# Loading the first row first, mask factors on 128 partitions on GpSimd, and list numbers converted inside the block loop

## The chip, the cores and the metric

One core of a Trainium2 chip runs one program. The metric is the device time of one execution in microseconds (us), as a median over runs. The engines are TensorE (PE in the profile; PEld is its weight load), VectorE (DVE), ScalarE (ACT), GpSimd (POOL) and SyncE (SP), which here only issues DMAs. They run side by side and wait for one another on semaphores.

## The reference, cut to what matters

x has 4 batch rows of 512 tokens and 128 features.

```python
x = x + 0.5 * ffn0(layernorm(x))        # 2 layers: local attention + gated FFN
x = x + attn(layernorm(x))              # 16 heads, with a mask of sines
x = x + 0.5 * ffn0(layernorm(x))        # the same weights again
x = x + 0.5 * mixture(x)                # 8 experts, 2 for each token, and a shared one
x = x + ttt(x)                          # two steps of training at test time
x = x + 0.5 * mixture(x)
```

Each head of `attn` adds 0.3 * log(sigmoid(val / temperature) + 1e-6) to its scores, with

```python
pos = arange(L) / L * 2 * pi
val = sin(pq) * cos(pk) + sin(pk) * cos(pz) + sin(pz) * cos(pq) - threshold
# pq = pos_q + phase[0],  pk = pos_k + phase[1],  pz = (pos_q + pos_k) / 2 + phase[2]
```

By the addition theorems val is a product of six rows of 512 for the queries and six for the keys of a head: the mask factors. They depend only on the 16 heads' phases and on sines and cosines of the positions, which are loaded as a table.

## The kernel before

x is kept transposed, features on partitions, tokens along the free axis. The stages run in the order load, ffn0, attn, ffn1, moe0, ttt, moe1. Each engine has its own list of instructions, in program order, and every stage begins with a wait for x_ready, which is raised when a row of x is finished in the stage before.

**Semaphores.** Counters start at START = 1. GpSimd raises every semaphore by one at the beginning, in alphabetical order; a wait for START + n is satisfied only after that and n increments.

**The start.** SP issues the loads in the order phase, pos, acol, aw, bv_row, xT, con, fcol, wqkv, rot, wo, w1, w2 (`load_sync`), then waits for the mask factors (mask_rows), stores them to DRAM (mask_q, mask_k), and issues the late loads and the filling of the mixtures' lists. VectorE (`load_dve`) runs `mask_factors`: twelve small instructions on the angles of the 16 heads, a sine on ScalarE (`load_act`, L1129), and then some 21 instructions of 512 columns on 16 partitions; after that the constants (`mean_w` from con, L1059; bf16 copies), and x_ready. The factors lie in the arena, the memory that ffn0 needs, so GpSimd's `ffn_zero_pads` (L1006 to L1014) and VectorE's ffn0 wait until both are stored (mask_stored). TensorE and ScalarE wait for the pads (pads_zero).

**ffn0.** Row 0 is normalised: the mean (`ln_mean`, L266), centring (L296), square, variance (L271), Ln and Exp for 1/std, scaling (L301). ScalarE makes the rounded part of wqkv for layer 0 (L718, ahead of the square), VectorE the rest (`low(0)`, L908). Then h_hi and h_lo, and the projections (`product`, L318 to L320), with rotation on VectorE (L760), squares on ScalarE, sums on GpSimd (`summed`, L938; `rotated`, L947 and L949) and the scaling (`scaled`, L773). ScalarE's copy for layer 1 comes before the first squares, VectorE's `low(1)` after the last scaling, and TensorE's first scores after that; `maxima` (L787) reads them. From there rows follow each other in a pipeline.

**attn.** SP loads, for each pass of two heads, the mask factors (L1319 and L1320, six rows of 512 each) and then the split queries and keys. TensorE multiplies the factors (L1401); the first pass can begin only when they are there, later ones are loaded a pass ahead.

**The mixture.** Tokens are scattered into blocks of 128, sorted by expert, and SP loads the 39 blocks in four groups, XGROUPS = ((0, 3), (3, 15), (15, 27), (27, 39)), a semaphore each (xg0_loaded to xg3_loaded). Column 128 of a block holds the number of the token slot to which its result goes. VectorE converts those numbers to integers for all four groups (L1963) and then begins the loop over blocks, whose first instruction clips the gate of block 0 (L1971). TensorE turns block j and projects it (L1711 to L1713); in turning block 3 it waits for group 1. GpSimd scatters the results with the numbers (L2031).

Of the kernel before, what the change touches and what calls it, by code (L numbers as in the profile page):

```python
# [25 lines left out]
P = 128  # L26
# [21 lines left out]
MF = 6  # L48

# [70 lines left out]
def position_tables():  # L120

    pos = (np.arange(L, dtype=np.float32) / np.float32(L) * np.float32(2 * np.pi)).astype(np.float64)
    t = np.stack([np.sin(pos), np.cos(pos), np.sin(pos / 2), np.cos(pos / 2)])
    return np.tile(t[None], (NH, 1, 1)).astype(np.float32)
# [17 lines left out]
def build(nc, I, out, stop=None):  # L142
    ctx = ExitStack()
    with ctx:
# [22 lines left out]

        PS = ctx.enter_context(nc.psum_tensor("PS", [P, 8, 512], F32))
# [3 lines left out]
        mq_dram = nc.dram_tensor("mask_q", (NH, MF, L), F32).ap()  # L172
        mk_dram = nc.dram_tensor("mask_k", (NH, MF, L), F32).ap()
# [64 lines left out]
        w2 = carve([DEPTH, 3, D])  # L238
        stage_memory(big)
# [149 lines left out]
        def ffn_pe(pe, f):  # L389
# [192 lines left out]
            pe.wait_ge(s("low_by_dve"), START + FFN_SPLITS * (f + 1))  # L582
            scores(0, 0)
# [9 lines left out]
        def ffn_act(act, f):  # L593
# [120 lines left out]
            if f:  # L714
                act.wait_ge(s("ffn_loaded"), START + 64)
# [3 lines left out]
            ln_act(e_input(f, 0), 3)  # L719
            entered(0)  # L720
            for w, hi, _ in weights[1:]:
                act.activation(hi, w, ACT.Copy).then_inc(s("weights_high"), 1)
            for j in range(PAIRS + 1):
                if j < PAIRS:
                    squares(0, j)
                if j:
                    rnorm(0, j - 1)
            exponentials(0, 0)
# [7 lines left out]
        def ffn_dve(v, f):  # L736
# [164 lines left out]
            if f:  # L901
                v.wait_ge(s("ffn_loaded"), START + 64)
# [7 lines left out]
            ln_centre(xT[:, 0, :], e_input(f, 0), 3)  # L910
            low(0)
            ln_scale(e_input(f, 0), c_one, c_zero, y[:, 0, :])
            entered(0)
            for j in range(PAIRS + 1):
# [4 lines left out]
            low(1)  # L919
            maxima(0, 0)  # L920
# [96 lines left out]
        stage_memory()  # L1017
        pos = carve([4, L])
        m_q = carve([MF, L])
        m_k = carve([MF, L])  # L1020
        m_t = carve([6, L])
        ang, turns, ang_f, sc = (carve([8]) for _ in range(4))
        turns_i = turns.bitcast(I32)
        phase = carve([8])
# [1845 lines left out]
```

## Time and profile before

| what | value |
|---|---|
| median of 3 runs | 2316.15 us (2303.26 to 2316.34) |
| profiled execution, its own time | 2330.29 us |
| its span, first to last instruction | 2328.1 us |
| mean granted TensorE clock | 0.890 of full |
| PE, DVE, ACT, POOL busy | 81%, 66%, 53%, 46% |
| chain that ended last | PE 34%, DVE 7%, ACT 6%, issue 5%, POOL 4%, DMA 2% |

The profile is of one execution, and its own time lies beside its span; the runs are executions without it. Busy shares are means over stages that have different limits. The chain is followed back from the last instruction to what released each step.

### The profile page before, as it was taken

Reading aid. Unit: us, or ns where it says so; the run is one execution under the profiler, and the core shown is the slowest. Engines: PE = TensorE matmul, PEld = TensorE weight load, DVE = VectorE, ACT = ScalarE, POOL = GpSimd, SP = SyncE. Lnnn points to the kernel's source line nnn. Section 1 sums busy time; section 2 is a strip of 40 time slices with the busy share of each in tenths; the row PEclk is TensorE's granted clock in tenths of the full one; section 3 lists DMA queues with packets and bytes.
Section 4 is the critical chain, followed back from the end, with each engine's and each line's share of the span. In section 5 each row is a group of like instructions: output and inputs, shape, how many; then the busy total and the mean of one; then the engine's idle time right before and its main releaser. Section 6 shows DMA issues by size and latency. Waiting matters only on the chain.

```text
span 2328.1 us, 42531 instructions
## 1 busy us (share of the span) xinstructions
PE 1876.3 (81%) x14557; PEld 1177.2 (51%) x14620; DVE 1547.5 (66%) x2455; ACT 1226.8 (53%) x2826; POOL 1062.6 (46%) x838
## 2 busy tenths in 40 slices
PE   2799999859898889569999985399569999884696
PEld 1456665424555555245556652288234554633485
DVE  5687778456979987468887864478445455426485
ACT  2467766437979997346667655144332332334242
POOL 2466566334767776346666551523223133005233
PEclk9799999876979997679999997699779999995797
DMA  6000000020000001000000003200400000000202
GB/s 230 1 1 2 2 2 1 1 92 13 25 19 21 22 26 44 10 1 2 2 2 2 2 2 111 79 19 22 150 0 0 1 0 0 1 0 27 63 23 70
DMA packets 43934, 63.40 MB, mean 27 GB/s; under 512 B 7504, under 2 KB 33488, under 8 KB 42736
## 3 DMA queue, kind: packets, MB, share of 16 engines
q1 hardware_dynamic: 39232, 51.96, 7.2%
q0 software_dynamic: 4544, 9.35, 1.2%
q8 instruction: 97, 1.59, 0.3%
q14 instruction: 61, 0.50, 0.1%
HBM read 45.26 MB, written 21.18 MB: 29 GB/s over the span
## 4 chain that ended last, share of the span: by engine, by line
PE 34%; DVE 7%; ACT 6%; issue 5%; POOL 4%; DMA 2%; SPq 0%; DVEq 0%; ACTq 0%; POOLq 0%
PE PS L1729 3%; POOL sorted_x L2024 3%; PE PS L1711 2%; PE PS L448 2%; ACT arena L635 1%; PE PS L1712 1%; PE PS L1713 1%; PE PS L2350 1%; PE PS L1719 1%; PE PS L2321 1%; PE PS L2367 1%; PE PS L2363 1%; DVE arena L760 1%; PE PS L2297 1%; PE PS L2371 1%
## 5 line engine op out<-in xcount | busy, mean ns | idle before, releaser
L1503 POOL TENSOR_TENSOR arena<-arena 128x1024 f32<-128x1024 f32 x128 | 299.6, 2362 | 144.2 <-ACT arena L1437 144.2
L635 ACT ACTIVATE arena<-PS,arena 128x128 f32<-128x128 f32 x512 | 180.2, 370 | 120.3 <-DVE arena L787 119.9
L955 POOL TENSOR_TENSOR arena<-arena 128x512 f32<-128x512 f32 x128 | 132.4, 1040 | 225.8 <-DVE arena L794 223.9
L1411 PE MATMUL PS<-con,arena 128*128 128x128 f32 x1024 | 163.5, 307 | 45.4 <-DVE arena L1487 44.0
L318 PE MATMUL PS<-arena_r 128*128 128x512 f32 x216 | 120.6, 558 | 92.5 <-DVE arena_r L1924 43.6
L760 DVE SCALAR_TENSOR_TENSOR arena<-PS,fcol,big 128x512 f32<-128x512 f32 x256 | 177.4, 741 | 15.8 <-PE PS L320 9.1
L1411 PEld LDWEIGHTS PS<-con,arena 128*128 128x128 f32 x1024 | 124.4, 155 | 121.1 <-issue 96.5
L1437 ACT ACTIVATE arena<-PS,arena 128x512 f32<-128x512 f32 x256 | 154.9, 688 | 56.3 <-DVE arena L1468 54.5
L1487 DVE COPY arena<-PS 128x512 f32<-128x512 f32 x256 | 166.2, 684 | 24.9 <-PE PS L1411 24.8
L1448 ACT ACTIVATE arena<-arena 128x512 f32<-128x512 f32 x256 | 162.6, 636 | 23.3 <-DVE arena L1475 17.2
L2031 POOL DMA_INDIRECT expert_y<-arena x78 | 74.7, 957 | 207.6 <-DVE arena L1990 203.9
L1468 DVE TENSOR_REDUCE arena<-PS 128x4 f32<-128x2048 f32 x64 | 146.6, 2291 | 29.3 <-PE PS L1393 29.3
L938 POOL TENSOR_TENSOR arena<-arena 128x512 f32<-128x512 f32 x64 | 109.3, 1708 | 67.6 <-ACT arena L611 30.8
L611 ACT ACTIVATE arena<-PS 128x512 f32<-128x512 f32 x128 | 74.1, 593 | 110.3 <-PE PS L320 77.0
L448 PE MATMUL PS<-arena 32*64 32x128 f32 x4096 | 131.6, 278 | 0.0
L1825 ACT ACTIVATE big<-big 128x512 f32<-128x512 f32 x78 | 49.3, 632 | 155.7 <-DVE big L1971 155.7
L448 PEld LDWEIGHTS PS<-arena 32*64 32x64 f32 x4096 | 115.7, 136 | 28.4 <-issue 28.4
L2465 POOL TENSOR_TENSOR arena<-arena 128x512 f32<-128x512 f32 x32 | 40.7, 1273 | 171.9 <-DVE arena L2412 171.8
L773 DVE SCALAR_TENSOR_TENSOR arena<-arena 128x512 f32<-128x512 f32 x128 | 116.2, 954 | 4.5 <-ACT arena L621 4.5
L787 DVE TENSOR_REDUCE arena<-PS 128x4 f32<-128x512 f32 x128 | 82.1, 682 | 50.1 <-PE PS L448 49.4
L318 PEld LDWEIGHTS PS<-arena_r 128*128 128x128 f32 x216 | 44.3, 205 | 133.6 <-DVE arena_r L1620 39.7
L635 ACT ACTIVATION_READ_ACCUMULATOR arena<-PS,arena 128x1 f32 x512 | 107.1, 209 | 0.0
(373 smaller groups left out, 4714.2 us busy)
## 6 DMA issues: line engine op xcount, KB each, us to landing
big<-in_gu SPq DMA_DIRECT2D x16, 512.0 KB, 8.4
sorted_x<-in_slots SPq DMA_DIRECT2D x2, 2515.5 KB, 14.5
arena<-sorted_x SPq DMA_DIRECT2D x6, 774.0 KB, 7.4
big<-in_dn SPq DMA_DIRECT2D x16, 256.0 KB, 8.7
arena<-expert_y SPq DMA_DIRECT2D x16, 256.0 KB, 3.3
big<-in_wqkv SPq DMA_DIRECT2D x2, 1536.0 KB, 8.6
arena<-q_split SPq DMA_DIRECT2D x96, 32.0 KB
arena<-k_split SPq DMA_DIRECT2D x96, 32.0 KB
```

Of the source, the lines that this page charges most:

```text
L318: pe.matmul(bank, w_hi, hi, start=first, stop=False)
L448: mm = pe.matmul(PS[w * WINDOW:(w + 1) * WINDOW, par, t * P:(t + 1) * P], qs[h, i, a:a + WINDOW], keys, start=False, stop=half == 1, skip_ ...
L635: act.activation(pr[:, u % 2, t, :], PS[:, u % 2, t * P:(t + 1) * P], ACT.Exp, bias=nmax[:, u % 2, t:t + 1], accum_out=psum_[:, u % 2, t:t ...
L760: v.scalar_tensor_tensor(t_prod[:, j % 2, 2 * half + i, :], PS[:, pair_bank(r, j) + half, :], fcol[:, layer, kind + half:kind + half + 1], ...
L773: v.scalar_tensor_tensor(dst, t_rn[:, j % 2, :], 1e12, t_rot[:, j % 2, half, :], ALU.min, ALU.mult).then_inc(s("qk_scaled"), 1)
L955: g.tensor_tensor(pn[:, u % 2, :, :], pr[:, u % 2, :, :], pinv[:, u % 2, :].unsqueeze(2).broadcast_to([P, TPB, P]), ALU.mult).then_inc(s(" ...
L1411: tr = pe.transpose(PS[:, 4 + t % 2, kt * P:(kt + 1) * P], pp[:, st % 2, t, kt * P:(kt + 1) * P], ident)
L1437: act.activation(pp[:, st % 2, t, :], PS[:, t, :], ACT.Exp, bias=a_nmax[:, st % 2, t:t + 1]).then_inc(s("a_exp"), 1)
L1448: act.activation(z, z, func, bias=bias, scale=scale).then_inc(s("mask_stage"), 1)
L1468: v.tensor_reduce(a_nmax[:, st % 2, :], PS[:, 0:TPB, :], AX.X, ALU.max, negate=True).then_inc(s("a_nmax"), 1)
L1487: v.tensor_copy(ppT[:, :, t * P:(t + 1) * P], PS[:, 4 + t % 2, :].rearrange("p (a b) -> p a b", a=TPB)).then_inc(s("ppT_ready"), 1)
L1503: g.tensor_tensor(a, a, mk[:, hp, 2 * half:2 * half + 2, :], ALU.mult).then_inc(s("a_masked"), 1)
```

## The change

Five edits, in the start and in the mixture.

1. `load_sync` loads row 0 of x, phase and pos first (first_loads), then layer 0 of wqkv and con (con_loaded), fcol and rot (rot_loaded), then layer 1 of wqkv, rows 1 to 3 of x, wo, w1 and w2 (ffn_loaded), then the attention's columns. SP raises 83 semaphores (LATE) to START itself; GpSimd raises 17 others (FIRST) before the remaining ones. `mean_w` becomes a memset.
2. phase and pos are laid out on 128 partitions: 16 heads x 8 chunks of 64 positions (CHUNKS, CW). VectorE keeps the twelve angle steps (`mask_angles`), then raises x_ready; ScalarE's sine follows; GpSimd computes the factors after the pads (`mask_factors(g)`), in 27 instructions of 64 columns, ahead of its first sum of ffn0. The factors lie in `big`, behind the weights, and no longer in the arena, so nothing of ffn0 waits for their store. In DRAM they are stored by chunk, and attention loads them in pieces of 64.
3. The waits of ffn0's first row are spread: TensorE takes the mean after first_loads and waits for pads, constants and con_loaded only before the projections; VectorE's `load_consts` stands between centring and `low(0)`; rot_loaded is waited for before the rotation, ffn_loaded before the first scores.
4. ScalarE squares before it copies layer 0 of wqkv, and copies layer 1 after the last rnorm. The columns from acol (`attn_consts`) are computed on VectorE before the first maxima.
5. In the mixture, the numbers of group g are converted in the block loop at block a + 1, where a is the group's first block.

```diff
-            sp.dma_start(phase[0:NH, :], I["phase"]).then_inc(s("phase_loaded"), 16)
-            sp.dma_start(pos[0:NH, :, :], I["pos"]).then_inc(s("phase_loaded"), 16)
...
+            sp.dma_start(xT[:, 0, :], I["xT"][:, 0, :]).then_inc(s("first_loads"), 16)
+            sp.dma_start(phase, I["phase"]).then_inc(s("first_loads"), 16)
+            sp.dma_start(pos, I["pos"]).then_inc(s("first_loads"), 16)
+            sp.dma_start(wqkv[:, 0, :], I["wqkv"][:, 0, :]).then_inc(s("con_loaded"), 16)
+            sp.dma_start(con[:], I["con"]).then_inc(s("con_loaded"), 16)
...
+            for name in LATE:
+                sp.sem_inc(s(name), START)
+            sp.wait_ge(s("mask_rows"), START + 1)
...
-            if f == 0:
-                g.wait_ge(s("mask_stored"), START + 32)
...
             if f == 0:
+                pe.wait_ge(s("first_loads"), START + 48)
             ln_pe(xT[:, 0, :], e_input(f, 0), 3, 3)
+            if f == 0:
+                pe.wait_ge(s("pads_zero"), START + 6)
+                pe.wait_ge(s("consts"), START + 7)
+                pe.wait_ge(s("con_loaded"), START + 32)
...
+            if f == 0:
+                ln_square(e_input(f, 0))
+                act.wait_ge(s("con_loaded"), START + 32)
             for w, hi, _ in weights[:1]:
                 act.activation(hi, w, ACT.Copy).then_inc(s("weights_high"), 1)
...
+            if f == 0:
+                act.wait_ge(s("ffn_loaded"), START + 80)
+                for w, hi, _ in weights[1:]:
+                    act.activation(hi, w, ACT.Copy).then_inc(s("weights_high"), 1)
             exponentials(0, 0)
...
             ln_centre(xT[:, 0, :], e_input(f, 0), 3)
+            if f == 0:
+                load_consts(v)
             low(0)
...
             low(1)
+            if f == 0:
+                attn_consts(v)
             maxima(0, 0)
...
             def angle_sum(dst, t, a, x, b, y, op):
-                then(v.tensor_scalar(t, a, x, None, ALU.mult))
-                then(v.scalar_tensor_tensor(dst, b, y, t, ALU.mult, op))
+                g.tensor_scalar(u, b, y, None, ALU.mult).then_inc(s("mask_step"), 1)
+                steps[0] += 1
+                then(g.tensor_scalar(t, a, x, None, ALU.mult))
+                then(g.tensor_tensor(dst, u, t, op))
...
-                sp.dma_start(mq_st[hp][0:MF], mq_dram[bass.ds(h, 1), :, :].rearrange("a f n -> (a f) n")).then_inc(s(f"factors{hp}_loaded"), 16)
+                sp.dma_start(mq_st[hp][0:MF].rearrange("f (c n) -> f c n", c=CHUNKS), mq_dram[bass.ds(h, 1), :, :, :].rearrange("a c f n -> f (a c) n")).then_inc(s(f"factors{hp}_loaded"), 16)
...
-            for g, (a, z) in enumerate(XGROUPS):
+            def block_ids(g):
+                a, z = XGROUPS[g]
                 v.wait_ge(s(f"xg{g}_loaded"), START + 16 * (m + 1))
                 v.tensor_copy(ids_u[:, a:z], xg[:, a:z, D]).then_inc(s("ids_ready"), 1)
...
+            turned_in(0)
+            turned_in(1)
             for u in range(NBLK + 3):
+                for g, (a, z) in enumerate(XGROUPS):
+                    if u == a + 1:
+                        block_ids(g)
...
                     ffn_zero_pads(g, f)
+                    if f == 0:
+                        mask_factors(g)
                     ffn_pool(g, f)
```

## Rows read from the trace of the kernel before

**Rows 1.** Busy time by stretch, the start: bounds, length, busy (count), granted clock, DMA, GB/s.
```profile
core 0: us, PE busy (x) PEld busy (x) DVE busy (x) ACT busy (x) POOL busy (x), PEclk, DMA share, GB/s
0.00:32.00 32.00, 0.00 (x0) 0.00 (x0) 15.86 (x52) 1.49 (x2) 1.40 (x10) 1.00 0.67 220
```

**Rows 2.** Timeline of the start: start us, us, engine, line, operation [idle before, releaser].
```profile
2.12 0.43 SPq L1031 DMA_DIRECT2D aw<-in_aw  x1
...
3.54 0.43 SPq L1033 DMA_DIRECT2D con<-in_con  x1
...
9.12 0.16 DVE L1082 COPY arena<-arena 16x3 f32<-16x3 f32 x1 [8.07 <-POOLq L2787]
...
11.59 0.21 ACT L1129 ACTIVATE arena<-arena 16x6 f32<-16x6 f32 x1 [9.56 <-DVE arena L1094]
...
30.68 0.15 POOL L1006 MEMSET arena<- 128x65 f32 x1 [30.24 <-DMA mask_k<-arena]
...
32.32 2.05 PE L266 MATMUL PS<-xT,mean_w 128*128 128x512 f32 x2 [32.32 <-POOL arena L1013]
...
33.57 1.48 ACT L718 ACTIVATE arena_r<-big 128x1536 fp32r<-128x1536 f32 x1
...
35.11 1.75 DVE L908 TENSOR_TENSOR big_r<-big,arena_r 128x1536 fp32r<-128x1536 f32 x1
...
39.40 0.75 DVE L301 SCALAR_TENSOR_TENSOR ln_scaled<-ln_centered,col,ln_rstd 128x512 f32<-128x512 f32 x1 [2.54 <-ACT ln_rstd L287]
...
42.87 0.77 PE L318 MATMUL PS<-arena_r 128*128 128x512 f32 x1 [4.88 <-issue]
...
47.08 1.28 POOL L938 TENSOR_TENSOR arena<-arena 128x512 f32<-128x512 f32 x1 [14.91 <-issue]
```

**Rows 3.** Timeline of the first mixture, where its block loop begins.
```profile
1503.05 0.17 DVE L1963 CAST arena<-arena 128x12 uint32<-128x12 f32 x1 [0.70 <-DMA arena<-sorted_x]
...
1503.62 0.63 PE L1713 MATMUL PS<-big_r,arena_r 128*128 x1
...
1508.39 0.17 DVE L1963 CAST arena<-arena 128x12 uint32<-128x12 f32 x1 [2.44 <-DMA arena<-sorted_x]
1508.48 0.69 DVE L1971 TENSOR_SCALAR big<-PS 128x512 f32<-128x512 f32 x1
```

**Rows 4.** Busy time by stretch, two stretches of attention's loop, columns as in rows 1.
```profile
540.00:560.00 20.00, 19.94 (x114) 11.14 (x114) 12.30 (x13) 14.07 (x25) 12.21 (x6) 0.50 0.03 6
580.00:600.00 20.00, 16.96 (x174) 10.14 (x173) 18.10 (x23) 19.09 (x34) 14.81 (x7) 1.00 0.10 27
```

**Rows 5.** DMA issues of the first 80 us: count, KB, us from issue to landing.
```profile
con<-in_con SPq DMA_DIRECT2D x1, 527.5 KB, 6.5
...
aw<-in_aw SPq DMA_DIRECT2D x1, 256.0 KB, 2.7
```

**Rows 6.** GpSimd's instructions by shape, whole span: count, busy us, mean ns, idle before.
```profile
L1503 POOL TENSOR_TENSOR arena<-arena 128x1024 f32<-128x1024 f32 x128 | 299.6, 2362 | 144.2 <-ACT arena L1437 144.2
L955 POOL TENSOR_TENSOR arena<-arena 128x512 f32<-128x512 f32 x128 | 132.4, 1040 | 225.8 <-DVE arena L794 223.9
...
L2282 POOL TENSOR_TENSOR arena<-arena 128x1024 f32<-128x1024 f32 x4 | 7.6, 1912 | 42.8 <-ACT arena L2177 42.8
...
L1009 POOL CAST arena_r<-arena 128x65 fp32r<-128x65 f32 x4 | 0.8, 237 | 0.1
```

**Rows 7.** Timeline of ffn0's first row: VectorE beside GpSimd, alone, and before maxima.
```profile
57.61 3.42 DVE L773 SCALAR_TENSOR_TENSOR arena<-arena 128x512 f32<-128x512 f32 x2 [0.68 <-ACT arena L621]
...
58.77 1.71 POOL L949 TENSOR_TENSOR arena<-arena 128x512 f32<-128x512 f32 x1
...
67.97 1.29 DVE L773 SCALAR_TENSOR_TENSOR arena<-arena 128x512 f32<-128x512 f32 x2 [0.20 <-ACT arena L621]
...
75.69 1.29 DVE L787 TENSOR_REDUCE arena<-PS 128x4 f32<-128x512 f32 x2 [4.77 <-PE PS L448]
```

**Rows 8.** Timeline of the start of attention's loop.
```profile
515.30 0.29 SPq L1320 DMA_DIRECT2D arena<-mask_k  x1
...
517.09 2.04 PE L1401 MATMUL PS<-arena 6*128 6x512 f32 x2 [15.11 <-DMA arena<-mask_k]
```

More of the change, by code:

```diff
@@ L238, in build @@
         w2 = carve([DEPTH, 3, D])
+        pos = carve([4, CW])
+        m_q, m_k = carve([MF, CW]), carve([MF, CW])
+        m_t = carve([6, CW])
+        ang, turns, ang_f, sc, phase = (carve([8]) for _ in range(5))
+        turns_i = turns.bitcast(I32)
         stage_memory(big)
@@ L582, in ffn_pe @@
             pe.wait_ge(s("low_by_dve"), START + FFN_SPLITS * (f + 1))
+            pe.wait_ge(s("ffn_loaded"), START + 80)
             scores(0, 0)
@@ L901, in ffn_dve @@
             if f:
-                v.wait_ge(s("ffn_loaded"), START + 64)
+                v.wait_ge(s("ffn_loaded"), START + 96)
             weights = ffn_weights()
@@ L1055, in load_dve, with load_consts @@
                 v.memset(col[:, i:i + 1], val).then_inc(s("columns"), 1)
-            mask_factors(v)
+            v.memset(mean_w[:], 1.0 / D).then_inc(s("consts"), 1)
+            mask_angles(v)
             v.wait_ge(s("columns"), START + 7)
-            v.wait_ge(s("first_loads"), START + 80)
-            v.tensor_scalar(mean_w[:], ones, 1.0 / D, None, ALU.mult).then_inc(s("consts"), 1)
+            v.tensor_copy(col[:, 7:8], c_one).then_inc(s("x_ready"), B)
+        def load_consts(v):
+            v.wait_ge(s("con_loaded"), START + 32)
             v.tensor_copy(ident_b[:], ident).then_inc(s("consts"), 1)
@@ L1080, in mask_factors @@
             two_pi_lo = float(2 * np.pi - two_pi_hi)
-            v.wait_ge(s("phase_loaded"), START + 32)
-            then(v.tensor_copy(ang[h, 0:3], phase[h, 0:3]))
-            then(v.tensor_scalar(ang[h, 3:6], phase[h, 0:3], pi / 2, None, ALU.add))
-            then(v.tensor_scalar(ang_f[h, 0:6], ang[h, 0:6], 1.0 / (2 * pi), None, ALU.mult))
-            then(v.tensor_copy(turns_i[h, 0:6], ang_f[h, 0:6]))
-            then(v.tensor_copy(ang_f[h, 0:6], turns_i[h, 0:6]))
+            v.wait_ge(s("first_loads"), START + 48)
@@ L1090, in mask_factors @@
             for op, bound, turn in ((ALU.is_gt, pi, -two_pi_hi), (ALU.is_lt, -pi, two_pi_hi)):
-                then(v.tensor_scalar(ang_f[h, 0:6], ang[h, 0:6], bound, turn, op, ALU.mult))
-                then(v.tensor_tensor(ang[h, 0:6], ang[h, 0:6], ang_f[h, 0:6], ALU.add))
-            then(v.tensor_scalar(ang[h, 0:6], ang[h, 0:6], 3.1415925, -3.1415925, ALU.min, ALU.max))
-            v.tensor_copy(sc[h, 6:7], ang[h, 0:1]).then_inc(s("angles"), 1)
-            v.wait_ge(s("sines"), START + 1)
@@ L1096, in mask_factors @@
-            s0, s1, s2, c0, c1, c2 = (sc[h, i:i + 1] for i in range(6))
-            sa, ca, sh, ch = (pos[h, i, :] for i in range(4))
-            def angle_sum(dst, t, a, x, b, y, op):
-                then(v.tensor_scalar(t, a, x, None, ALU.mult))
-                then(v.scalar_tensor_tensor(dst, b, y, t, ALU.mult, op))
-            t = m_t[h, 5, :]
-            sin_q, cos_q, sin_z, cos_z, sin_k = m_q[h, 0, :], m_t[h, 1, :], m_t[h, 2, :], m_q[h, 1, :], m_t[h, 4, :]
+                then(v.tensor_scalar(ang_f[:, 0:6], ang[:, 0:6], bound, turn, op, ALU.mult))
@@ L2785, in _ @@
         def _(g):
-            for name in sorted(set(sems) - {"x_scattered", "y_scattered"}):
-                g.sem_inc(sems[name], START)
+            names = [n for n in sorted(sems) if n not in FIRST + LATE + ("x_scattered", "y_scattered")]
+            for name in FIRST + tuple(names):
+                g.sem_inc(s(name), START)
             for st in run:
```

146 lines of the change are left out of this document (92 added, 54 removed).

## Prediction

> **What bounds the kernel now.** I read four views, in this order. The table of busy time by stretch comes first: in the first 32.0 us TensorE does nothing (x0) and VectorE is busy for half [rows 1]. So the 81% of TensorE over the whole span says nothing about the start, and what is saved there is saved in full, since each later stage waits for the x of the one before it.
>
> The timeline of the start says what those 32 us are [rows 2]. VectorE's first piece of the mask factors stands until 9.12 us, and what released it is GpSimd's queue: GpSimd raises every semaphore to START in alphabetical order, and phase_loaded comes late in it. Sines follow at 11.59, then the 512-wide factors on 16 partitions, their store, and only when mask_k has landed (30.24) does GpSimd zero the pads from 30.68. TensorE's first layer-norm matmul starts at 32.32, the first projection at 42.87, GpSimd's first sum of squares at 47.08.
>
> The third view is the timeline at the first mixture [rows 3]. The half-row of block 0 that is clipped first has its last matmul at 1503.62 + 0.63 = 1504.25, but the clip (L1971) starts at 1508.48, because VectorE stands in the list-number casts of groups 1 to 3; the last of them starts at 1508.39, released by its load. Group 1, which TensorE needs for block 3, was there at 1503.05. The second mixture repeats this.
>
> The fourth is the table by stretch inside attention, for the noise [rows 4]. Two stretches of 20 us with the same loop: granted clock 1.00 (2.4 GHz) with 23 VectorE instructions, granted 0.50 (1.2 GHz) with 13. A low stretch so costs about 20 x (1 - 13/23) = 8.7 us.
>
> **The change, part by part.** Times are on the profiled execution: 2330.29 us, span 2328.1.
>
> *First row first.* The new gate is first_loads: row 0 of x, phase, positions, 0.40 MB, the first three issues; its START is GpSimd's first increment instead of about its hundredth. In the trace, aw is the load with 0.39 MB up to and with it: issued 2.12, landed 2.7 later, 4.8 us [rows 2, 5]. I take 4.8. The upper bound is con, with 2.0 MB up to it: 3.54 + 6.5 = 10.0 (if the loads issued behind share the engines with the first ones). The angle steps stay on VectorE, 12 small instructions, 11.59 - 9.12 = 2.5 us, whose length hardly hangs on 16 or 128 partitions; x_ready follows them, so TensorE's mean starts at about 7.4 instead of 32.3. From there to the first projection it was 42.87 - 32.32 = 10.55 us, and the chain (mean, square, variance, rstd, scale, halves) is the same. So 18.0 without disturbance.
>
> *Waits that are added in it.* con_loaded (weights of layer 0 and con, 1.7 MB up to it) lands before 10.0 by the con row. ScalarE reaches it after its square at about 11, with the weight copy and rstd queued behind it; VectorE reaches it after the centring at 10.3, with low(0) and the scaling behind. Zero cost, at most 2 us if the loads are slower than con's. low(0) loses its lead: the copy (1.48, L718) now comes after the square, so low(0), 1.75 us, ends about 0.3 before the scaling can start, where it had 39.40 - 36.86 = 2.5 to spare. rot_loaded and ffn_loaded (6 MB in all) are needed at about 20 and 48; by 32.0 us the core had moved 220 GB/s x 32 us = 7.0 MB [rows 1]. Zero.
>
> *Mask factors on GpSimd.* 27 instructions of 64 columns on 128 partitions, after the pads (1.6 us, 30.68 to 32.3), so from 9.0. No row shows a TENSOR_SCALAR on GpSimd. From the rows [rows 6]: a 65-wide cast 0.24; a two-input one, from 1040 ns at 512 and 1912 at 1024, 1.70 ns a column, 0.28 at 64. The 17 one-input ones at 0.24 and 10 two-input ones at 0.28 make 6.9 us. Twenty of them are waited for; VectorE's 13 angle instructions of 0.16 fill 2.47 us, a gap of 0.03, and I take twice that, 1.2. Together 8.1 us, done at 17.1. It must be done by the first sum, 4.2 us after the projection.
>
> *VectorE beside it.* Two two-input operations in SBUF take 1.29 us when GpSimd is idle and 3.42 beside GpSimd's adds of 1.28 to 1.71 us [rows 2, 7]: each loses 1.07, close to one GpSimd instruction. On the path, about six VectorE instructions (low(0), scale, add, cast, two subtractions) can meet GpSimd; with GpSimd's instructions a quarter of a us long, 6 x 0.25 = 1.5 us. Lower bound 0; upper bound all the GpSimd work still to come when low(0) starts, 8.1 - 3.4 = 4.7. The projection so comes at 19.5, and the prologue gives 42.87 - 19.5 = 23.4. GpSimd is held up in turn, at most by low(0) and all from the scaling to the projection, 1.75 + (42.87 - 39.40) = 5.2 us, and six small casts of con at the 0.17 of rows 3, 1.0: done by 23.3 at worst, needed at 23.7. Hidden, barely.
>
> The Trainium skill (SBUF — State Buffer, section Who interferes with whom) speaks against this part: a VectorE operation with two SBUF inputs and a GpSimd operation that reads SBUF lock each other out, one whole instruction at a time. By that rule six instructions wait at most one short GpSimd instruction each, an estimated 1.7 us together, and 1.7 would stand in place of the 4.7 as the bound: the sum would be -31.1 at worst of this part, not -28.1. The rows point the same way (1.07 lost beside adds of 1.28), but with long instructions only.
>
> *Layer 1's weights later.* ScalarE's copy (1.48) now starts after the last rnorm, at the time of VectorE's last two scalings (1.29): low(1) and the first scores come 0.2 later (0 to 1.5). The three tiny acol instructions stand before maxima, where VectorE waits 4.77 us for TensorE anyway [rows 7]; without that cover they cost 0.5.
>
> *SP.* 83 increments and later mask stores on its queue: the stores move from 25 to about 20, the late loads behind them too, and nothing before attention at 515 asks for them. The factor loads become 256-byte pieces, 48 instead of 6 each. At attention's start TensorE waits for mask_k, 515.30 to 517.09 [rows 8]: I add 0.3 (0 to 1.8, the wait doubled). Later passes load a pass ahead.
>
> *Mixtures.* The clip goes from 1508.48 to 1504.3: 4.2 each, 8.4 together; the loop behind it is a chain of blocks, so it is kept. What stands behind a cast in VectorE's queue now is a clip, and behind that TensorE; the casts of groups 1 to 3 come at blocks 4, 16 and 28, when their loads (the last at 1508.39) are long there or, for block 4, three blocks old. Four casts of 0.17 cost at most 0.7 per mixture, if VectorE is the late one. Bounds per mixture 3.5 to 5.6: TensorE also loses a stall of some 4 us and may reach the high clock a block or two sooner.
>
> Sum: -23.4 + 0.2 + 0.3 - 8.4 = -31.3. 2330.29 becomes 2299.0. The median of the runs shown lies 14.1 below the profiled execution, less than two low stretches of rows 4; taken off it, 2316.15 - 31.3 = 2284.9, say 2285.
>
> **Rivals.** *The prologue gives less.* GpSimd is late for its first sum: the price decides from (23.7 - 9.0)/27 = 0.54 us an instruction. At 1.04 (the 512-wide adds of L955) it is done at 37, 13 late, and the result is 2298. A first load at 10.0 instead of 4.8 gives 2290. For it: no TENSOR_SCALAR row, the tight slack. Against: the 0.24 of the cast.
>
> *The mixture gives nothing*, because the first blocks then wait for something else (group 1 in turn_in, a cast): 2293. Against: group 1 was there at 1503.05.
>
> *Slower.* One mechanism: GpSimd's 27 factor instructions, in the place before its first sum. At 1.71 each (L949 beside VectorE) they end at 55.2, 31.5 late, and the whole gain is eaten; above that the kernel is slower. At the dearest row, 2.36 (L1503), they end at 72.7, 49 late: 2334. Against: that is the price of 1024 columns, here there are 64. That the change doesn't do what it says is the same case, the wait for the mask moved from VectorE to GpSimd.
>
> **How the numbers follow.** Forecast 0.72, less prologue 0.17, no mixture 0.05, slower 0.03; 0.03 for more than bounds allow. The range joins the sum's own bounds (-36 to -24: the 4.7, 1.8, 1.5 and the casts one way, no disturbance and a sooner clock the other) and one low stretch more or less, some 8 us: 2270 to 2300, which takes in the first two rivals. A change under 1%, 23 us, is what a measurement here hardly tells from none; the forecast is 1.35%, so a low stretch or two can bring it below. Of the forecast's 0.72 some 0.65 stays above 1%, of the first two rivals half, of the rest up 0.03: faster 0.79, same 0.19, slower 0.02.
>
> **What would show it.** Right: TensorE's first matmul at 7 to 8, first projection at 18 to 21, GpSimd's factors done before its first sum, first clip in each mixture within 5 us of the first list load. Wrong: GpSimd busy with factors when ScalarE's squares are done; first_loads later than 6; con_loaded ending ScalarE's wait; the interval from projection to attention longer than in rows 2 to 8; TensorE waiting for xg1.

## The result, and the profile after

The changed kernel takes 2274.9 us (median of 4 runs, 2272.9 to 2277.3), beside 2315.8 for the kernel before (2303.3 to 2316.3): ratio 0.9837, 95% interval 0.9802 to 0.9872. That ratio is the one of the mean times, which lie 37.8 us apart; the two medians lie 40.9 apart. The forecast was 2285, range 2270 to 2300, a gain of 31.3. The direction, the range and both mechanisms held; 6.5 us of the 37.8 are not in the forecast, and the experiments are mostly about them.

The stretch that answers to [rows 1], busy time by stretch of the changed kernel's start, same columns: TensorE works 14.40 of the 32 us instead of none, and GpSimd 22.63 instead of 1.40.

```profile
0.00:32.00 32.00, 14.40 (x32) 7.70 (x32) 18.84 (x46) 11.01 (x15) 22.63 (x43) 1.00 0.70 251
```

The timeline of the same start answers to [rows 2].

```profile
5.04 0.17 DVE L1135 COPY big<-big 128x3 f32<-128x3 f32 x1 [3.83 <-DMA big<-in_pos]
...
7.62 2.04 PE L288 MATMUL PS<-xT,mean_w 128*128 128x512 f32 x2 [7.62 <-DVE col L1105]
...
9.25 0.45 POOL L1164 TENSOR_SCALAR big<-big 128x64 f32<-128x64 f32 x1
...
12.53 1.76 DVE L949 TENSOR_TENSOR big_r<-big,arena_r 128x1536 fp32r<-128x1536 f32 x1 [1.13 <-ACT arena_r L750]
12.54 2.05 POOL L1166 TENSOR_SCALAR big<-big 128x64 f32<-128x64 f32 x1
14.66 0.88 DVE L323 SCALAR_TENSOR_TENSOR ln_scaled<-ln_centered,col,ln_rstd 128x512 f32<-128x512 f32 x1 [0.38 <-ACT ln_rstd L309]
...
18.74 0.77 PE L340 MATMUL PS<-arena_r 128*128 128x512 f32 x1 [5.50 <-issue]
...
21.74 1.09 ACT L640 ACTIVATE arena<-PS 128x512 f32<-128x512 f32 x2 [4.90 <-PE PS L342]
...
23.72 0.15 POOL L1185 MEMSET big<- 128x64 f32 x1
23.83 1.27 POOL L987 TENSOR_TENSOR arena<-arena 128x512 f32<-128x512 f32 x1
```

The first matmul moved from 32.32 to 7.62, the first projection from 42.87 to 18.74, 24.1 earlier, and GpSimd's first sum from 47.08 to 23.83, 23.25 earlier. The last three lines show the 0.9 us between these two: ScalarE's first squares are done at 22.83, and the sum starts the moment the last factor instruction is done, without idle time before it. TensorE's projection would have let it start at 18.74 + 4.21 = 22.95, with the 4.21 of [rows 2].

The forms of GpSimd between 9 and 24 us, which answer to the prices of [rows 6]:

```profile
L1166 POOL TENSOR_SCALAR big<-big 128x64 f32<-128x64 f32 x6 | 4.8, 806 | 0.0
L1164 POOL TENSOR_SCALAR big<-big 128x64 f32<-128x64 f32 x6 | 3.5, 585 | 0.6
L1167 POOL TENSOR_TENSOR big<-big 128x64 f32<-128x64 f32 x6 | 2.0, 329 | 0.5
...
L1183 POOL COPY big<-big 128x64 f32<-128x64 f32 x1 | 0.2, 237 | 0.1
```

A TENSOR_SCALAR of 64 columns in the angle sums (L1164, L1166) is nearly twice as dear as a copy of that size, 0.43 to 0.45 us where nothing meets it, and one of them stands 2.05 us.

The timeline of the first mixture answers to [rows 3]: the first projection (L1773), the last matmul of the first half-row (L1775), the clip (L2037), the first cast (L2026), now behind the clip, and the next transpose.

```profile
1459.48 0.79 PE L1773 MATMUL PS<-arena_r 128*128 x1
...
1460.49 0.63 PE L1775 MATMUL PS<-big_r,arena_r 128*128 x1
...
1461.16 0.69 DVE L2037 TENSOR_SCALAR big<-PS 128x512 f32<-128x512 f32 x1 [1.94 <-PE PS L1775]
...
1462.92 0.16 DVE L2026 CAST arena<-arena 128x3 uint32<-128x3 f32 x1
...
1463.15 0.45 PE L1760 MATMUL PS<-con,arena 128*128 128x128 f32 x1 [0.75 <-DVE arena_r L2020]
```

In the kernel before, the first projection and the next transpose of the same place:

```profile
1502.61 0.79 PE L1711 MATMUL PS<-arena_r 128*128 x1
...
1510.47 0.45 PE L1698 MATMUL PS<-con,arena 128*128 128x128 f32 x1 [4.93 <-DVE arena_r L1958]
```

The clip comes right behind that matmul, as its releaser says, instead of 4.2 us after it. From the first projection to the next transpose it is 1463.15 - 1459.48 = 3.67 us, and was 1510.47 - 1502.61 = 7.86: 4.2 less. In the second mixture the same two instructions stood at 2170.61 and 2178.31 and stand at 2121.16 and 2124.83: 4.0 less. From the clip of block 0 to that of block 38 it takes 118.3 to 119.3 us in the traces of the two kernels that convert all numbers up front (before, and prologue only, below) and 117.5 to 119.3 in those of the list-number edit alone and of the changed kernel, so what is won at the first clip is neither lost nor multiplied in the loop.

The start of attention, for [rows 8]: from the issue of mask_k's load to the first mask matmul 2.16 us instead of 1.79. In the other traces of kernels that load these factors in pieces at this place it is 1.86 to 2.14, so the pieces cost 0.1 to 0.4 us.

```profile
487.53 0.28 SPq L1382 DMA_DIRECT2D arena<-mask_k  x1
...
489.69 2.04 PE L1463 MATMUL PS<-arena 6*128 6x512 f32 x2 [15.50 <-DMA arena<-mask_k]
```

And two stretches in attention, for [rows 4]; the loop still has stretches at 0.50 with few VectorE instructions and stretches near 1.00 with many:

```profile
540.00:560.00 20.00, 18.74 (x109) 10.12 (x108) 12.79 (x13) 11.20 (x21) 9.11 (x5) 0.50 0.04 9
560.00:580.00 20.00, 17.77 (x169) 10.80 (x168) 17.64 (x22) 16.45 (x30) 13.34 (x6) 0.93 0.09 24
```

So the sum of the places that the edits touch is 23.25 + 4.2 + 4.0 - 0.4 = 31.1 us in the two traces, against 31.3 forecast and 37.8 measured.

### The profile page after: what moved, and what is told of

It reads as the page before. It is cut to its first block, busy times and chain, and to the rows that moved or that the text cites. A ratio compares the mean times of both kernels' runs of the same rounds, so it can differ in the third digit from the quotient of the medians.

```text
span 2275.5 us, 42539 instructions
## 1 busy us (share of the span) xinstructions
PE 1850.7 (81%) x14557; PEld 1165.6 (51%) x14620; DVE 1530.8 (67%) x2433; ACT 1227.7 (54%) x2826; POOL 1078.4 (47%) x865
## 4 chain that ended last, share of the span: by engine, by line
PE 35%; DVE 9%; issue 6%; ACT 6%; POOL 1%; DMA 1%; DVEq 0%; SPq 0%; ACTq 0%; POOLq 0%
PE PS L1791 3%; PE PS L1773 2%; PE PS L470 2%; PE PS L1775 2%; PE PS L1774 2%; PE PS L2416 1%; DVE arena L801 1%; PE PS L1781 1%; PE PS L2387 1%; ACT arena L664 1%; PE PS L2433 1%; PE PS L2429 1%; PE PS L2363 1%; PE PS L2437 1%; PE PS L504 1%
## 5 line engine op out<-in xcount | busy, mean ns | idle before, releaser
L664 ACT ACTIVATE arena<-PS,arena 128x128 f32<-128x128 f32 x512 | 180.7, 370 | 119.6 <-DVE arena L828 119.3
L1473 PE MATMUL PS<-con,arena 128*128 128x128 f32 x1024 | 157.2, 298 | 48.4 <-DVE arena L1549 46.0
L1473 PEld LDWEIGHTS PS<-con,arena 128*128 128x128 f32 x1024 | 118.8, 150 | 121.4 <-issue 94.6
L814 DVE SCALAR_TENSOR_TENSOR arena<-arena 128x512 f32<-128x512 f32 x128 | 111.1, 914 | 5.1 <-ACT arena L650 5.1
```

Source lines behind the costliest of these rows:

```text
L664: act.activation(pr[:, u % 2, t, :], PS[:, u % 2, t * P:(t + 1) * P], ACT.Exp, bias=nmax[:, u % 2, t:t + 1], accum_out=psum_[:, u % 2, t:t ...
L1473: tr = pe.transpose(PS[:, 4 + t % 2, kt * P:(kt + 1) * P], pp[:, st % 2, t, kt * P:(kt + 1) * P], ident)
```

## The experiments

The theory: each edit gives what its own stall was, and the rest of the 37.8 comes from TensorE's granted clock, whose mean differs from run to run. The rivals: the mixtures give the rest; the two edits together give more than each alone; the rest of the prologue (waits, load order) gives it.

To tell the clock from the edits I use the span and mean granted clock of every run. With the two levels of [rows 4], 1.00 and 0.50, the time at the low one is span x (1 - clock) / 0.5: of a run with 2293.9 and 0.905, it is 436 us. Over the 122 runs of the kernel before, the changed kernel and the eleven variants below, a straight line with one slope for all and a level for each row of the table fits to 2.0 us (the first comparison's runs of before, whose clocks are not known, are left out). Its slope is 0.354 us of run time for each us at the low clock; that is a fit over runs, and none of them set the clock. The last column is a kernel's level on this line at 450 us of low time, good to about 1 us.

| kernel | median us (runs) | ratio to before, 95% | mean low time, us | level at 450 us low |
|---|---|---|---|---|
| before, the runs beside the variants | 2306.4 (44) | | 458 | 2304.9 |
| changed, first runs | 2274.9 (4) | 0.9837 (0.9802 to 0.9872) | 444 | 2277.0 |
| changed, beside four variants | 2273.0 (6) | 0.9846 (0.9807 to 0.9884) | 435 | 2277.9 |
| list numbers only | 2295.6 (12) | 0.9960 (0.9934 to 0.9985) | 442 | 2299.7 |
| prologue only | 2284.0 (6) | 0.9909 (0.9885 to 0.9932) | 446 | 2284.1 |
| start held back | 2293.7 (9) | 0.9958 (0.9934 to 0.9982) | 434 | 2300.3 |
| alphabetical increments | 2283.5 (4) | 0.9879 (0.9826 to 0.9932) | 455 | 2282.3 |
| factors on VectorE | 2278.2 (4) | 0.9857 (0.9803 to 0.9910) | 435 | 2283.1 |
| factors twice | 2284.0 (10) | 0.9894 (0.9862 to 0.9927) | 451 | 2285.2 |
| x_ready early, factors split | 2268.8 (6) | 0.9849 (0.9820 to 0.9877) | 436 | 2273.9 |
| mask loads early | 2263.7 (4) | 0.9824 (0.9749 to 0.9898) | 423 | 2273.3 |
| both early | 2254.7 (4) | 0.9774 (0.9713 to 0.9835) | 398 | 2270.3 |
| TensorE kept busy | 2273.5 (5) | 0.9864 (0.9825 to 0.9903) | 434 | 2282.1 |
| both early, kept busy | 2260.4 (4) | 0.9804 (0.9764 to 0.9843) | 419 | 2271.8 |

The level is no clean measure of an edit: where TensorE's waiting itself lies at the low clock, taking it away takes low time away too, and the line books 0.354 of that to the clock. Both places are named below. The ratio and its interval come from all runs, and are not the quotient of the two medians. With four to six runs the interval is some 11 to 34 us wide, so few of these edits can be told apart by their medians; what follows rests on the traces and on the levels.

**List numbers only.** The kernel before with this edit alone:

```diff
-            for g, (a, z) in enumerate(XGROUPS):
+            def block_ids(g):
+                a, z = XGROUPS[g]
                 v.wait_ge(s(f"xg{g}_loaded"), START + 16 * (m + 1))
                 v.tensor_copy(ids_u[:, a:z], xg[:, a:z, D]).then_inc(s("ids_ready"), 1)
-                if g == 0:
-                    turned_in(0)
-                    turned_in(1)
+
+            turned_in(0)
+            turned_in(1)
             for u in range(NBLK + 3):
+                for g, (a, z) in enumerate(XGROUPS):
+                    if u == a + 1:
+                        block_ids(g)
```

> The kernel before with only the list-number edit. Theory (each edit gives what its own stall was, and the 6.5 us beyond the forecast come from where TensorE's low clock falls in attention): the two mixtures give the 4.3 and 3.1 us read from the two traces, 7.4 together, so 2308 from a median of 2316, give or take the 8 us of one low stretch. Rival (the excess comes from the mixtures, which are worth all that the start does not give, 37.8 - 23.3 = 14.5): 2301.

Measured: 2295.6, below both forecasts, which started from 2316. It is 11.2 below the 2306.8 of the 20 runs of before beside it; the interval is 3.5 to 15.2 and holds the theory's gain and the rival's. The timeline of the first mixture shows the same clip as in the changed kernel, 1.68 us behind the projection's start:

```profile
1478.68 0.79 PE L1711 MATMUL PS<-arena_r 128*128 x1
...
1480.36 0.69 DVE L1975 TENSOR_SCALAR big<-PS 128x512 f32<-128x512 f32 x1 [1.94 <-PE PS L1713]
...
1482.35 0.30 PE L1698 MATMUL PS<-con,arena 128*128 128x128 f32 x1 [0.75 <-DVE arena_r L1958]
```

The 3.67 us from projection to transpose are 7.86 in the kernel before, as in the changed one. The level falls by 5.2. Here a part is booked to the clock, as busy time by stretch of the kernel before shows, one stretch of 2 us in the stall of each mixture:

```profile
1506.00:1508.00 2.00, 0.00 (x0) 0.00 (x0) 0.00 (x0) 0.00 (x0) 0.00 (x0) 1.00 0.90 217
...
2174.00:2176.00 2.00, 0.00 (x0) 0.00 (x0) 0.00 (x0) 0.00 (x0) 0.00 (x0) 0.50 0.80 193
```

No engine works in either, and the second stall lies at 0.50, the first only at its ends. So between 4.0 and 8.2 us of low time go with the stalls, 1.4 to 2.9 at 0.354, and 6.6 to 8.1 in all. Of the 14.5 that the rival needed, the place itself shows none beyond 8.2; the median alone would not have told them apart.

**Prologue only.** The changed kernel with the first diff turned round.

> The changed kernel with the list numbers converted up front again, as in the kernel before. Theory (as for the run of the list-number edit alone): 2275 + 7.4 = 2282, and 23 to 33 below the kernel before. Rival (the excess comes from the mixtures): 2275 + 14.5 = 2289. Rival (the two edits are not additive, because a moved start shifts where the low clock falls): any time further than 8 us from 2282.

Measured: 2284.0, 22.8 below before (interval 15.7 to 26.5), level 20.8 below. 22.8 and 11.2 are 34.0 in the medians, against the 33.8 of both edits in the next run; the levels give 20.8 + 5.2 = 26.0 against 27 to 28. So the two edits add, as far as 2 us at equal clock can be told from none.

**The changed kernel beside them.**

> The changed kernel once more, beside the others on one chip. Theory (the 37.8 us of the first comparison were 6 us too many, because the runs of the kernel before that it was held against lay high: 2316 there, 2307 in the 20 runs beside the single edits): the gain is 21 + 9 to 11 = 30 to 32, 0.987. Rival (the two edits together give more than each alone): 36 us and more, 0.984 or less.

Measured: 2273.0, 33.8 below the 2306.9 of the 17 runs beside it, interval 26.8 to 44.5. That lies between the theory's 30 to 32 and the rival's 36, and the interval holds both. But the kernel before has been run 44 times by now: 2298.9 to 2327.8, median 2306.4, where the four runs of the first comparison had 2315.8. Against 2306.4, the 2274.9 and 2273.0 are gains of 31.5 and 33.4, nearer to the theory.

**Start held back.** One instruction and its wait in the changed kernel, ahead of the angle steps:

```diff
+            v.memset(arena[:, 0:27000], 0.0).then_inc(s("columns"), 1)
+            v.wait_ge(s("columns"), START + 8)
             mask_angles(v)
-            v.wait_ge(s("columns"), START + 7)
```

> The changed kernel with one VectorE memset of 27000 columns ahead of the angle steps, so that TensorE's first matmul should come near 32 us instead of 7.6, as in the kernel before; all else stays. Theory (the start is on the path in full): the time grows by the same 24 us, to 2299, give or take one low stretch of 8, and that is 9 below the kernel with the list-number edit alone, which would then be what the rest of the prologue and the clock give. Rival (later stages wait for something else, a load or a store, so that the start is worth less than its length): under 2290.

```profile
6.79 22.56 DVE L1103 MEMSET arena<- 128x27000 f32 x1 [5.57 <-issue]
...
31.95 2.04 PE L288 MATMUL PS<-xT,mean_w 128*128 128x512 f32 x2 [31.95 <-DVE col L1106]
...
516.54 2.04 PE L1464 MATMUL PS<-arena 6*128 6x512 f32 x2 [15.46 <-DMA arena<-mask_k]
```

Everything starts 24.3 us later (the projection at 43.02), as late as in the kernel before, and attention's first mask matmul, 516.54 instead of 489.69, is 26.9 later. Measured: 2293.7, 19 to 21 above the two medians of the changed kernel, level 22.8 above (2277.5, the mean of its two, here and below). It lies where the list-number edit alone lies (2295.6, levels 2300.3 and 2299.7). So the start is worth 19 to 23 of its 24.3 us at the end, and of the prologue nothing but its earlier start gives anything that can be seen beside the 1 us of a level: the rival that waits and load order gave the rest is out.

**Alphabetical increments.** The changed kernel without FIRST and LATE:

```diff
-            for name in LATE:
-                sp.sem_inc(s(name), START)
...
-            names = [n for n in sorted(sems) if n not in FIRST + LATE + ("x_scattered", "y_scattered")]
-            for name in FIRST + tuple(names):
+            for name in sorted(set(sems) - {"x_scattered", "y_scattered"}):
                 g.sem_inc(s(name), START)
```

> The changed kernel with every semaphore raised by GpSimd in alphabetical order again, as in the kernel before, so that x_ready comes last. Theory (the order of these increments is a part of the gain by itself): the queue that reached phase_loaded at 9.1 us in the kernel before reaches x_ready at 12 to 14, the first matmul moves from 7.6 to there, and the end with it: 2279 to 2282. Rival (the loads and the angle steps set the start, the increments are hidden): first matmul below 8.5, 2275 to 2276.

```profile
12.40 2.04 PE L288 MATMUL PS<-xT,mean_w 128*128 128x512 f32 x2 [12.40 <-POOLq L2852]
```

The first matmul at 12.40 is released by GpSimd's queue, 4.8 later; the level is 4.8 higher, the median 8.6 to 10.5, above the 2279 to 2282 expected. The order and place of these increments were worth some 5 us of the gain.

**Factors on VectorE.**

```diff
             mask_angles(v)
+            mask_factors(v)
...
-                    if f == 0:
-                        mask_factors(g)
```

> The changed kernel with the 27 factor instructions of 64 columns on VectorE, right behind the angle steps and ahead of x_ready, none on GpSimd. Theory (a GpSimd instruction of this size costs 0.54 us with its wait, a VectorE one about 0.2 by the angle steps, but all of it stands on the path here): the first matmul 5.5 to 6.5 later, at 13.1 to 14.1, the first sum 0.9 less late and the scaling undisturbed, so the first sum 3.5 to 5 later and the time 2279 to 2280. Rival (contention between VectorE and GpSimd costs the changed kernel more than its own rows show): 2275 or less.

```profile
14.08 2.05 PE L288 MATMUL PS<-xT,mean_w 128*128 128x512 f32 x2 [14.08 <-DVE col L1106]
...
25.00 0.77 PE L340 MATMUL PS<-arena_r 128*128 128x512 f32 x1 [5.29 <-issue]
...
29.22 1.28 POOL L987 TENSOR_TENSOR arena<-arena 128x512 f32<-128x512 f32 x1 [13.63 <-issue]
```

The first matmul comes 6.5 later and the first sum 5.4; the level is 5.6 higher, the median 3 to 5. This run also prices the contention: with GpSimd idle, mean to projection takes 25.00 - 14.08 = 10.92; beside its factors, 18.74 - 7.62 = 11.12. Sharing cost VectorE's chain 0.2 us. The 10.92 is itself 0.37 above the 10.55 of the kernel before, and what adds that is open.

**Factors twice.** (The second time overwrites the first with the same numbers.)

```diff
...
-                        mask_factors(g)
+                        mask_factors(g, 0)
+                        mask_factors(g, 1)
```

> The changed kernel with GpSimd computing the mask factors twice over, 27 more instructions of 64 columns before its first sum of squares. Theory (GpSimd's factors stand on the path, since they end 0.9 us after the first sum could run): 27 at 0.44 to 0.54 us, the first sum at 36 to 38 instead of 23.8, and the end later by the same 12 to 14.6: 2287 to 2290. Rival (the lateness is absorbed by the 11 us in which GpSimd waits behind row 0's sums): the first sum moves, the end does not: 2275 to 2279.

```profile
34.48 1.26 POOL L987 TENSOR_TENSOR arena<-arena 128x512 f32<-128x512 f32 x1
...
499.94 2.04 PE L1466 MATMUL PS<-arena 6*128 6x512 f32 x2 [15.20 <-DMA arena<-mask_k]
```

The first matmul of this execution is at 6.65, so the first sum comes 27.8 behind it instead of 16.2: the second 27 took 0.43 us each. From the first matmul to attention's first mask matmul it is 499.94 - 6.65 = 493.3 us in this trace, and 479.9 to 482.2 in three traces with the factors computed once (the changed kernel's two and prologue only): 11.1 to 13.4 more, so close to all of the 11.6 arrives there, and the 11 us in which GpSimd later waits don't absorb it. Measured 2284.0, between theory and rival, 9 to 11 above the changed kernel, and the level 7.7 above. The rest of the 11.6 may be booked to the clock: up to attention this trace has some 70 us of low time against some 60, 3.5 at the slope of the line. GpSimd is on the path here, though at 0.43 an instruction, not the 0.54 of the theory's upper end.

**x_ready early, factors split.**

```diff
-            sp.wait_ge(s("mask_rows"), START + 1)
+            sp.wait_ge(s("mask_rows"), START + 2)
...
-            mask_angles(v)
             v.wait_ge(s("columns"), START + 7)
             v.tensor_copy(col[:, 7:8], c_one).then_inc(s("x_ready"), B)
+            mask_angles(v)
...
                     if f == 0:
-                        mask_factors(g)
+                        mask_factors(g, 0)
...
+            if f == 0:
+                mask_factors(g, 1)
             for r in range(ROWS):
```

> The changed kernel with x_ready raised before the angle steps, so that TensorE's mean runs beside them, and with the mask factors in two parts: four of the six angle sums before GpSimd's first sum of squares, the other 15 instructions behind row 0's sums, where GpSimd stood idle from 44 to 55 us. Theory (GpSimd's factors are 0.9 us late for the first sum, and the angle steps cost 2.3 on the path): first matmul at 5.1, first projection at about 17, first sum 2 to 3 us sooner than 23.83; 2272. Rival (the lateness is hidden by what follows, or the second part gets in VectorE's way): 2275 or more.

```profile
17.15 0.76 PE L340 MATMUL PS<-arena_r 128*128 128x512 f32 x1 [5.31 <-issue]
...
21.37 1.28 POOL L987 TENSOR_TENSOR arena<-arena 128x512 f32<-128x512 f32 x1 [5.22 <-issue]
```

GpSimd now waits 5.22 us for its first sum, which stands 4.22 behind the projection, as it did before the change. It is 2.46 sooner; the level is 3.6 lower, the median 4 to 6. That speaks against the rival, but doesn't rule it out: the interval of this run, 2265 to 2278, reaches its 2275, and attention's first mask matmul at 487.67 lies where three traces with the unsplit factors have it, 487.5 to 489.7.

**Mask loads early.** The last lines of the profile after show another wait: TensorE is idle for 15.5 us at attention's start, and the load that ends it stands in SP's queue behind the stores of the split keys. The first pass's factor loads go ahead of row 2's stores:

```diff
             for b in range(B):
+                if b == 2:
+                    sp.wait_ge(s("mask_stored"), START + 32)
+                    for hp in range(HEADS_PER_PASS):
+                        load_mask_factors(sp, 0, hp)
...
-            sp.wait_ge(s("mask_stored"), START + 32)
...
-                load_mask_factors(0, hp)
```

> The changed kernel, but the two heads' mask factors for attention's first pass are loaded while the projections of rows 2 and 3 run, instead of behind the last store of the split keys. Theory (at attention's start TensorE waits for mask_k alone, 483.4 to 489.7 us): its first mask matmul comes 5 to 6 us sooner, near 484, and as the heads land near 492, before the four mask quarters are through, the end comes 5 to 6 sooner: 2268 to 2269. Rival (the heads' loads, still behind the stores, are then what ends last): 2 or less, 2272 to 2274.

```profile
480.42 2.04 PE L1464 MATMUL PS<-arena 6*128 6x512 f32 x2 [9.61 <-DVE arena L1345]
```

The wait is now for VectorE's last values and 9.61 long instead of 15.50. Median 2263.7, 9 to 11 below the changed kernel, but over four runs from 2247 to 2280; the level falls by 4.2, somewhat short of the 5 to 6 expected.

**Both early.** The last two diffs together.

> The kernel with x_ready raised early and the factors split, with the early loads of mask factors on top. Theory: the two gains add, 3.5 and 5 to 6 at equal time at the low clock, so 2264 to 2265 and the fastest of all. Rival: the loads gain nothing and it stays at 2269.

Measured: 2254.7, ratio 0.9774 (0.9713 to 0.9835), level 2270.3: 52 below the kernel before, 18 to 20 below the changed one, and the fastest kernel here. Only 7 of these 18 to 20 stand at equal low time; the other part goes with 37 to 46 us less of it. Whether that is owed to the edits, or is luck of four runs, is open.

**TensorE kept busy.** The changed kernel, with work that no one reads in the gap at attention's start:

```diff
         def attn_pe(pe):
+            for _ in range(12):
+                pe.matmul(PS[:, 7, :], mean_w[:], xT[:, 0, :], start=True, stop=True)
```

> The changed kernel with 12 matmuls of 128x512 (mean_w with row 0 of x, into bank 7, which the first mask matmul then overwrites) between the last projection and attention's first mask matmul, where TensorE stood idle for 15.5 us. Theory (what differs between runs of one kernel is the time at the granted clock of 0.50, at 0.34 us for each us of it, and the 37 us of it at attention's start follow from that idle time): the stretch from 478 to 515 shows a clock of 1.00 for a half of it or more, and the time falls by 6 to 13 us, to 2261 to 2268. Rival (the clock falls there whatever TensorE does before, or the low time is only put off): 2273 or more.

The timeline of TensorE, and then busy time by stretch at attention's start, the last two lines further on:

```profile
473.58 10.47 PE L1447 MATMUL PS<-xT,mean_w 128*128 128x512 f32 x24
489.61 2.04 PE L1465 MATMUL PS<-arena 6*128 6x512 f32 x2 [5.57 <-DMA arena<-mask_k]
```

```profile
480.00:500.00 20.00, 11.80 (x18) 3.50 (x16) 5.96 (x9) 7.14 (x12) 2.47 (x3) 0.67 0.30 92
500.00:520.00 20.00, 17.25 (x81) 7.78 (x81) 13.74 (x15) 18.40 (x31) 10.03 (x5) 0.64 0.00 0
520.00:540.00 20.00, 18.32 (x155) 10.24 (x154) 15.53 (x17) 17.53 (x32) 14.44 (x7) 0.78 0.09 24
540.00:560.00 20.00, 18.74 (x109) 10.12 (x108) 12.79 (x13) 11.20 (x21) 9.11 (x5) 0.50 0.04 9
560.00:580.00 20.00, 19.05 (x142) 11.13 (x144) 14.53 (x19) 13.25 (x25) 11.24 (x6) 0.69 0.08 20
```

The clock falls all the same, 10 us later: the stretches of 20 us from 480 to 560 have 0.67, 0.64, 0.78, 0.50 (the changed kernel 0.50, 0.62, 0.81, 0.50), and that from 560 has 0.69 where the changed kernel has 0.93. The median is 2273.5, that of the changed kernel, and the sign that the theory asked for, a clock of 1.00 over half of the stretch from 478 to 515, is not there. But the filler ends at 484.05 and leaves 5.57 of the idle us before the mask matmul, and stretches of 2 us show that the clock falls in these, as it fell in the idle time of the changed kernel. The changed kernel first, then this one:

```profile
474.00:476.00 2.00, 0.19 (x2) 0.00 (x1) 1.95 (x2) 1.05 (x1) 1.86 (x3) 1.00 0.81 262
476.00:478.00 2.00, 0.00 (x0) 0.00 (x0) 1.94 (x3) 0.00 (x0) 1.60 (x3) 0.90 0.08 25
478.00:480.00 2.00, 0.00 (x0) 0.00 (x0) 1.97 (x3) 0.00 (x0) 1.86 (x3) 0.50 0.59 192
```

```profile
484.00:486.00 2.00, 0.04 (x1) 0.00 (x0) 0.00 (x0) 0.00 (x0) 0.00 (x0) 1.00 0.82 267
486.00:488.00 2.00, 0.00 (x0) 0.00 (x0) 0.00 (x0) 0.00 (x0) 0.00 (x0) 0.73 0.26 87
488.00:490.00 2.00, 0.39 (x1) 0.42 (x2) 0.00 (x0) 0.00 (x0) 0.00 (x0) 0.50 0.28 78
```

So this run doesn't show that the clock falls whatever TensorE does before, and a filler that leaves no idle time was not tried. What it shows is that the low time saved here buys nothing. It was saved while attention's start waited for mask_k, and the first mask matmul stands at 489.61 as it stood at 489.69; behind it the clock is 0.50 up to 514 in both traces. The rival's other half, put off, fits the stretch from 560, and the mean low time, 434 us, is not below the changed kernel's 435 and 444. The level is 4 to 5 higher; 10 us of low time moved to a place where they cost 0.354 each would be 3.5 of it, but that is argued, not shown.

**Both early, kept busy** (8 such matmuls).

> The kernel with both early edits and 8 such matmuls between the last projection and the first mask matmul. Theory: 6 to 13 us below the kernel with both early edits alone, 2252 to 2259. Rival: the low time is put off and it is within 3 us of that kernel.

Measured: 2260.4, level 2271.8, against 2254.7 and 2270.3: no gain here either. 2.75 us without a matmul were left in front of the first mask matmul, and the clock fell between 478 and 482 again (0.72 over these 4 us, 1.00 before, 0.50 behind).

## Why the prediction was right, point by point

**Prologue, -23.4.** Right: 23.25 at the first sum in the traces, 22.8 in the median of the prologue alone. Holding the start back by 24.3 gave 19 to 23 back, so nothing later hid much of it. Inside, three terms were mis-sized and cancelled, so that the sum fits to 0.2 us is luck. First_loads landed at 5.04 where 4.8 was taken (4.07 and 4.33 in two other executions, so this term varies by a us). Contention was put at 1.5 and took 0.2: 11.12 against 10.92 without it. And GpSimd's factors were put at 8.1 us, done at 17.1, and took 14.6, done at 23.9. The step that failed is "The 17 one-input ones at 0.24": twelve of them are TENSOR_SCALARs that cost 0.43 to 0.45 undisturbed. Of the 6.5 us by which the factors were too short, 3.5 are this price (27 took 11.6 in the second pass of factors twice) and 3.0 the loss beside VectorE, for which the text had allowed up to 6.2. The mean, 14.6 / 27 = 0.54, is the price at which the first rival was said to decide, and it did begin: GpSimd was still at the factors when ScalarE's squares were done at 22.83, which the text had named as a sign of being wrong, and the first sum came 0.9 late. The worst case of the text, done by 23.3 and hidden barely, was nearer than the value taken, though for another reason.

**What the two engines do to each other.** The text looked for the loss on VectorE. The trace has it on GpSimd: VectorE's low(0) took its usual 1.76 (1.75 in [rows 2]), and the TENSOR_SCALAR issued beside it took 2.05 instead of 0.44. The Trainium skill (SBUF — State Buffer, section Who interferes with whom) says that such a pair lock each other out for a whole instruction. This pair agrees: GpSimd's instruction began 0.01 us behind VectorE's and ended 0.30 us behind its end. Whether GpSimd lost because it came second or because its instructions are short, one pair can't tell.

**Mixtures, -8.4.** Right: 4.2 and 4.0 in the traces, the clip where it was said to come, and the casts off the path: VectorE stands idle before none of the eight, and in the second mixture the clip comes 0.45 us after the instruction that precedes the cast (2136.56 to 2137.01), where without a cast it comes 0.43 to 0.44 after it. The noise was larger than the term: 11.2 in the median of this edit alone, interval 3.5 to 15.2.

**Small terms.** The factor loads in 256-byte pieces: 0.3 forecast, 0.37 in these two traces, 0.1 to 0.4 over all. Layer 1's weights and the acol instructions: the lead of 23.25 at the first sum hardly shrinks on the way through row 0 (before's maxima are at 75.69 [rows 7], after's at 52.61: 23.1, which is 0.2 less, as forecast).

**The forecast time.** 2285 against 2274.9. The gain was right, the base was not: the step that failed is "2316.15 - 31.3". The three runs it was taken from lay high; 44 more have their median at 2306.4, and 2306.4 - 31.3 = 2275.1. What goes with the difference between runs is time at the granted 0.50: the profiled execution of before, 0.890 on a span of 2328.1, had 512 us of it, the 44 runs 458 on average, and 54 x 0.354 = 19 us is most of the 24 between them. The clocks of the three runs are not known, so that they lay high for this reason is not shown. The text named one low stretch of 8 us as the noise; in the 44 runs of the kernel before it is 29 from end to end.

**What stays open.** For the two profiled executions the account nearly closes: 512 - 451 = 61 us of low time at 0.354 are 22, with the 31.1 of the places 53, of which 1.4 to 2.9 are counted twice; the spans differ by 52.6. At equal low time the levels differ by 27 to 28, to which 1.4 to 2.9 of the mixtures' stalls come back: 28 to 31. The changed kernel's runs also have 14 to 23 us less low time on average than those of before, of which the stalls themselves are 4 to 8. Whether the rest is owed to the edits or to where the stretches happen to fall is not settled, nor what makes the clock fall in attention: it fell in idle time of TensorE at attention's start, but the filler that was to take this time away left a third of it.

## What to carry to other kernels

A stall at the very start, with nothing beside it, was worth 19 to 23 of its 24.3 us at the end: look first at what the first instruction waits for, and there at the order in which semaphores are raised, worth some 5 us here for a list of names. A helper engine that takes work off the path has its own first deadline; price its instructions by a row of the same operation, not of the same size only, and count how long it may take. And before a gain of 1% is explained by edits, run the kernel before often enough to know its own spread, and compare runs at equal clock.

## What was not expected of the hardware

- GpSimd's TENSOR_SCALAR on 128x64 took 0.43 to 0.45 us undisturbed in the angle sums (0.37 and 0.51 in two other lines), where a COPY of that shape took 0.24, a TENSOR_TENSOR 0.32 and a MEMSET 0.15.
- A us more at the granted clock of 0.50 went with 0.354 us more of run time over 122 runs of these kernels, and the 44 runs of the kernel before lay between 2298.9 and 2327.8 with 432 to 507 us of it.
- With 10.5 us of filler matmuls at attention's start, TensorE's clock fell 10 us later, in the 5.57 us of idle time that the filler left, and the time stayed the same.
- The landing of the first loads moved by 1 us between executions (4.07 to 5.08 in the traces of the changed kernel and its variants).
